# Attention, mixing and expert stages of one network layer on one core: scores and first expert layer in one product, expert table split in two parts, query rows scaled by GpSimd, and a new order on every engine

## What is computed

```
y  = clip(modulated(x, cond) + bias, -256, 256)
q  = l2norm(layernorm(y) @ Wq) * q_scale;  k = l2norm(y @ Wk) * k_scale;  v = y @ Wv     # 16 heads of 64
x1 = x + softmax(8 * q k^T + alibi, causal, 2 null keys) @ v @ Wout
kx = modulated(x1, cond);  A = softmax(kx_h kx_h^T / 4) over the 16 heads of one row
z  = modulated(A kx, cond)
cluster = argmax(calibrate(z @ cluster_sigs^T))             # 8 clusters
tile    = argmax(calibrate(z @ sigs^T) inside cluster)      # 64 experts, 8 to a cluster
h  = gelu(z @ w1 + b1);  comp = tanh(h @ w2 + b2)           # 64 hidden, 2 out
mag = relu(comp @ spline_w1[tile] + spline_b1[tile]) @ spline_w2[tile] + spline_b2[tile]
out = x1 + layernorm(z + mag * directions[tile] * scale) * gamma + beta
```

## Time and profile before

| | |
|---|---|
| median of 3 runs | 1919.03 us (1913.91 to 1920.64) |
| profiled execution | 1920.77 us, of which 1919.0 us are the span from its first to its last instruction |
| PE busy | 1836.4 us (96%) |
| PEld busy | 1489.1 us (78%) |
| DVE busy | 1629.5 us (85%) |
| ACT busy | 1237.6 us (64%) |
| POOL busy | 1065.0 us (56%) |
| chain that ended last | PE 93%, DVE 4%, POOL 1%, ACT 1% |
| granted PE clock | 0.977 of full speed over the span |

### The profile page before, as it was taken

How to read it: one execution, slowest core, us unless ns; L and a number is a source line. 1 busy time by engine, 2 the same in 40 slices (tenths; PEclk the granted TensorE clock), 3 DMA queues, 4 the chain that set the end, 5 groups by cost and what they waited for, 6 DMA issues and landing times.

```text
span 1919.0 us, 63488 instructions
## 1 busy us (share of the span) xinstructions
PE 1836.4 (96%) x25286; PEld 1489.1 (78%) x25286; DVE 1629.5 (85%) x4120; ACT 1237.6 (64%) x2514; POOL 1065.0 (56%) x775
## 2 busy tenths in 40 slices
PE   4899999999999999999999999999999999999974
PEld 3688888878888887887888888788888878878762
DVE  5577888888888899888889888888988988898765
ACT  2566676666667666666766666666666676666642
POOL 0455565565565566556556655655655565565522
PEclk7899999999999999999999999999999999999985
DMA  4011122122112112112211211221121121122121
GB/s 145 9 26 37 41 46 46 40 42 44 39 44 44 37 42 44 44 38 46 42 38 44 44 44 38 41 45 40 44 44 39 40 44 44 38 47 43 44 48 28
DMA packets 337972, 83.09 MB, mean 43 GB/s; under 512 B 277007, under 2 KB 336879, under 8 KB 337903
## 3 DMA queue, kind: packets, MB, share of 16 engines
q1 hardware_dynamic: 337902, 82.12, 19.6%
HBM read 48.51 MB, written 33.55 MB: 43 GB/s over the span
## 4 chain that ended last, share of the span: by engine, by line
PE 93%; DVE 4%; POOL 1%; ACT 1%; issue 1%; SPq 0%; DMA 0%; POOLq 0%; ACTq 0%; DVEq 0%
PE pa L439 29%; PE ps L518 6%; PE pa L446 6%; PE pb L418 6%; PE ps L505 6%; PE ps L469 5%; PE ps L476 4%; PE pc L652 3%; PE pc L538 3%; PE pa L418 3%; PE ps L562 3%; PE pb L425 3%; PE pb L610 3%; PE pb L513 2%; PE ps L520 2%; PE pb L430 2%
## 5 line engine op out<-in xcount | busy, mean ns | idle before, releaser
L1106 POOL TENSOR_TENSOR yve<-ymv,eps 128x1 f32<-128x1 f32 x64 | 12.1, 190 | 547.3 <-DVE ymv L1007 547.3
L439 PE MATMUL pa<-wq,xnTs 128*128 128x512 f32 x768 | 213.4, 414 | 0.0
L439 PE MATMUL pa<-wv,y 128*128 128x512 f32 x768 | 210.4, 410 | 1.9 <-ACT kn L782 0.3
L439 PE MATMUL pa<-wk,y 128*128 128x512 f32 x768 | 211.8, 411 | 0.0
L1098 POOL TENSOR_TENSOR rn<-nrg,mhalf 128x16 f32<-128x16 f32 x64 | 203.4, 3177 | 4.2 <-DVE nrg L1055 3.7
L1086 POOL TENSOR_TENSOR rn<-nrg,mhalf 128x16 f32<-128x16 f32 x64 | 186.6, 2915 | 17.7 <-DVE nrg L1033 11.6
L439 PEld LDWEIGHTS pa<-wv,y 128*128 128x128 f32 x768 | 134.8, 188 | 32.3 <-issue 5.4
L1091 POOL TENSOR_TENSOR bd<-vm,pick 128x1024 f32<-128x1024 f32 x64 | 121.9, 1905 | 65.3 <-PE pc L652 61.5
L439 PEld LDWEIGHTS pa<-wq,xnTs 128*128 128x128 f32 x768 | 137.4, 192 | 24.9 <-ACT kcat L736 0.3
L439 PEld LDWEIGHTS pa<-wk,y 128*128 128x128 f32 x768 | 134.7, 188 | 27.8
L1103 POOL TENSOR_TENSOR pr<-pr,rden 128x1056 f32<-128x1056 f32 x64 | 135.9, 2123 | 2.9 <-DVE rden L927 2.9
(11 more groups left out here) (222 smaller groups left out, 5206.1 us busy)
## 6 DMA issues: line engine op xcount, KB each, us to landing
xT<-in_xT SPq DMA_DIRECT2D x64, 128.0 KB, 2.4
x<-in_x SPq DMA_DIRECT2D x64, 128.0 KB, 2.1
x1d<-x SPq DMA_DIRECT2D x64, 128.0 KB, 1.7
kxdr<-kxn SPq DMA_DIRECT2D x64, 128.0 KB, 1.7
vm<-kxdr SPq DMA_DIRECT2D x128, 64.0 KB, 2.8
odr<-o SPq DMA_DIRECT2D x256, 32.0 KB, 2.0
on<-odr SPq DMA_DIRECT2D x64, 128.0 KB, 2.1
xb<-x1d SPq DMA_DIRECT2D x64, 128.0 KB, 2.1
```

The costliest lines, as they stand in the source:

```text
L439: last = mm(bank, part(lhs(a_, k)), part(rhs(b_, k)), start=(n == 0), stop=(n == 3 * CK - 1))
```

## The change

Four edits of the work, and new lists for all engines:

1. Scores and first expert layer become one product: zT as weights against all 136 columns of `wsc`. The hidden layer is then in rows (`hidn`). For each two tiles PE transposes it once; gelu reads the result with b1 as its bias, and one product with a block-diagonal `w2b` serves both tiles. b2 becomes the bias of two tanh instructions.
2. `gath` is split once, in the setup, into a high and a low part (`gath2`, one column wider, which holds zeros). The product with `ohT` becomes two float32r products.
3. The query rows are scaled by GpSimd, between the two powers.
4. The lists: the q and k products move from tile i-1 to i-2, the attention scores from i-2 to i-3, `kx` from i-4 to i-5, the one-hot and table product from i-8 to i-9, and so on; the low parts of y move from the end of y's own step into the next.

```diff
+        hidn = sb("hidn", [P, 2, CH])
+        hT = sb("hT", [2 * CH, P])
+        gath2 = sb("gath2", [NT, 2, GATH + 1])
...
PE, tile i-7:
-                    for k in range(CK):
-                        mm(pb[:, C:C + NS], zT[:, k, :], wsc[:, k, 0:NS],
-                           start=(k == 0), stop=(k == CK - 1), skip_group_check=True)
-                    for k in range(CK):
-                        last = mm(pb[0:CH, C + P:C + 2 * P], wsc[:, k, NS:NS + CH], zT[:, k, :],
-                                  start=(k == 0), stop=(k == CK - 1), skip_group_check=True)
+                    for k in range(CK):
+                        last = mm(pb[:, C:C + NS + CH], zT[:, k, :], wsc[:, k, :],
+                                  start=(k == 0), stop=(k == CK - 1), skip_group_check=True)
...
+                if live(i, 8):
+                    if p == 1:
+                        nc.tensor.transpose(pb[:, C:C + P], hidn[:, :, :].rearrange("p u h -> p (u h)"), ident[:, :])\
+                            .then_inc(S("hT_mm"), 2)
...
-                        for u in range(2):
-                            mm(pb[:, C + P + 2 * u:C + P + 2 * u + 2], hT[:, u, :], w2b[:, :], start=True, stop=True)
+                    if 1 - p == 0:
+                        mm(pb[:, C + P:C + P + 4], hT[:, :], w2b[:, :], start=True, stop=True)
...
-                    mm(pb[:, 0:GATH], ohT[:, :], gath[:, :], start=True, stop=True).then_inc(S("gathered"), 1)
+                    for a in range(2):
+                        last = mm(pb[:, 0:GATH + 1], part(ohT[:, :]), part(gath2[:, a, :]), start=(a == 0), stop=(a == 1))
...
ACT:
-                    fn(hT[0:CH, 1 - p, :], pb[0:CH, C + P:C + 2 * P], ACT.Identity, bias=b1[:, :]).then_inc(S("hidden"), 1)
+                    fn(hidn[:, 1 - p, :], pb[:, C + NS:C + NS + CH], ACT.Copy).then_inc(S("hidden"), 1)
...
+                    if p == 1:
+                        fn(hT[:, :], pb[:, C:C + P], ACT.Gelu, bias=b1[:, :]).then_inc(S("gelu_done"), 2)
...
+                    if 1 - p == 0:
+                        for o in range(2):
+                            fn(comp[:, :, o], pb[:, C + P:C + P + 4].rearrange("p (u o) -> p o u", o=2)[:, o, :], ACT.Tanh,
+                               bias=b2[:, o:o + 1])
...
DVE:
-                if live(i, 2):
-                    wait(dve, "q_rsqrt", t2)
-                    v.tensor_tensor(by_head(qn), by_head(qn), bc(rn[:, 0, :], 2, DH), ALU.mult).then_inc(S("qn_done"), 1)
...
POOL, after the power of the query norms:
+                    wait(pool, "q_rsqrt", t2)
+                    g.tensor_tensor(by_head(qn), by_head(qn), bc(rn[:, 0, :], 2, DH), ALU.mult).then_inc(S("qn_done"), 1)
+                    wait(pool, "k_guard", t2)
+                    g.tensor_tensor(rn[:, 1, :], nrg[:, 1, :], mhalf[:, :], ALU.pow).then_inc(S("k_rsqrt"), 1)
```

More of the change, by code:

```diff
@@ L355, in step @@
                     sp.dma_start(plain(x1d, t4), x1[:, p, :]).then_inc(D("x1_out", p), 16)
[L356 to L362, removed]
-                    for u in range(2):
[L364 to L372, removed]
+                if live(i, 3):
+                    if live(i, 5):
+                        wait_dma(sp, "x1_out", t5, 1 - p)
+                    sp.dma_start(x1[:, 1 - p, :], plain(x_t, t3)).then_inc(D("x_in", 1 - p), 16)
             pipeline(sp, step)
@@ new lines, in step @@
+                if live(i, 2):
+                    wait(pe, "q1_raw", t2)
+                    project(pa[:, 1, :], lambda a, k: y3f[:, p, a, k, 0:P],
+                            lambda a, k: wk[:, a, k, 1 * 512:2 * 512]).then_inc(S("k1_mm"), 1)
+                if live(i, 3):
+                    for s in range(BT):
+                        last = sim_tile(R7, 1, s)
+                    last.then_inc(S("sim_mm"), 1)
+                if live(i, 6):
+                    wait(pe, "aT_done", t6)
+                    wait(pe, "spread", t6)
@@ new lines, in step @@
+                if live(i, 2):
+                    wait(pe, "q0_raw", t2)
+                    project(pa[:, 0, :], lambda a, k: y3f[:, p, a, k, 0:P],
+                            lambda a, k: wk[:, a, k, 0 * 512:1 * 512]).then_inc(S("k0_mm"), 1)
+                if live(i, 6):
+                    for n in range(G):
+                        for u in range(2):
+                            half, b4, c4 = n % 2, n // 2, 2 * (n % 2) + u
+                            g = half * G8 + b4
+                            at = b4 // QG * P + half * DH + b4 % QG * H
+                            rows = slice(u * DH, (u + 1) * DH)
+                            last = mm(pc[c4 * DP:(c4 + 1) * DP, b4 * DH:(b4 + 1) * DH],
+                                      aT[rows, at:at + DP], vbd[rows, :, g * DM:(g + 1) * DM],
+                                      start=True, stop=True, skip_group_check=True)
+                    last.then_inc(S("av_mm"), 1)
@@ L482, in step @@
+                if live(i, 4):
+                    for r in range(4):
+                        mm(ps[:, 2, C:2 * C], oT[:, r, :], wout[:, r, :], start=(r == 0), stop=False)
+                if live(i, 9):
+                    wait(pe, "ohT_done", t9)
+                if live(i, 7):
+                    linear_T(two(pb, C), wo2, om).then_inc(S("zT_mm"), 1)
                 if live(i, 2):
@@ L541, in step @@
                     last.then_inc(S("mix_scores"), 1)
[L542 to L549 removed]
                 if live(i, 2):
+                    wait(pe, "qT1_done", t2)
@@ L571, in step @@
-                if live(i, 4):
-                    wait(pe, "kxT_done", t4)
-                    from_T(two(pb, 0), kxT).then_inc(S("kxn_mm"), 1)
+                        for t, s in ((0, 0), (1, 1), (1, 0), (0, 1)):
+                            last = pv_tile(r, t, s, 1 - p)
+                    last.then_inc(S("pv_mm"), 1)
                 if live(i, 5):
@@ L681, in _ @@
             loaded(act, "late_in")
+            fn(part(gath2[:, 0, 0:GATH]), gath[:, :], ACT.Copy).then_inc(S("gath_high"), 1)
             act.wait_ge(S("nullw_mm"), 1)
```

620 lines of the change are left out of this document (302 added, 318 removed).

## The result

The changed kernel takes 1999.18 us (median of 4 runs, 1997.54 to 2001.10), the kernel before 1918.44 in the same session. The ratio is 1.0424 (95% interval 1.0402 to 1.0447): 4.2% slower. 1959 was forecast, within a range of 1868 to 2022. The direction held; the loss is 81 us, twice the 40 that were forecast, and just above the likeliest case's own range, 1925 to 1995.

What follows compares the result with a forecast made beforehand. PE bounds the kernel before at 28.15 us a step; DVE would bound the changed one at 29.0. From 1920.8, +47 over 55 steps and -7 at the ends give 1961, as median 1959; range 1868 to 2022.

Steps and rivals of the forecast that it cites:

- the likeliest case: DVE bound, with DVE's subtraction ahead of POOL's query product: 1959 us, own range 1925 to 1995, chance 0.46.
- PE's saving: Per step: fused scores and hidden layer 0.52, expert table 0.29, two-tile hidden layer costs 0.03; together 0.78 us.
- the lock: DVE instructions with two SBUF inputs and POOL instructions reading SBUF, powers excepted, exclude each other; the first holds until it ends.
- (c): After the key-norm power: POOL's division, xb and key rows in a row delay DVE's chain gs to yy by 3.8 us.
- The four places: Spots in the new lists where DVE waits for POOL's holds: 1.2, 0.6, 3.8 and 0.9 us a step.
- DVE's step: 22.5 us without the waits for POOL, 29.0 with them, more than PE's 27.4 and the old 28.15.
- The step that failed: Filling and draining steps: DVE and POOL seldom collide, PE's saving counts for some nine tiles, -7 us.
- PE stayed the bound: Rival: DVE's waits add up to less than 4.9 us, PE's saving shows, 1869 us (1860 to 1890); chance 0.23.
- The race at (b): After q_guard, DVE's subtraction leads POOL's query product by 0.1 us; rival: POOL first, +1.3 a step, 2031 or 1995; chance 0.17.
- The powers: Rival: GpSimd's powers, which read SBUF, hold DVE up too; 253 us more, about 2210; chance 0.01.
- (a): After y_mv: POOL's spread holds 1.89 us and DVE stands 1.2 us before the division of the mixing weights.

Runs made afterwards that it cites:

- run 5: Kernel before, in its own order, plus both product edits and nine small products in PE's set-up that move its loop: 1876.83 us, ratio 0.9780.
- run 8: Changed kernel with the old expert-table product (two passes of 321 columns) put back: 2002.89 us, ratio 1.0437.
- run 1: Changed kernel with GpSimd's softmax division, addition of beta and key-row scaling replaced by powers of about the same length: 1890.21 us, ratio 0.9857.
- run 7: Changed kernel with GpSimd's xb and key rows held until VectorE has copied the null keys, in the first 12 steps only: 1994.30 us, ratio 1.0395.
- run 9: Changed kernel with xb and key rows held until the null-key copy, and the spread until the one-hot rows are written: 1925.03 us, ratio 1.0034.
- run 10: Changed kernel with only GpSimd's spread held until VectorE has written the one-hot rows: 1987.48 us, ratio 1.0359.
- run 6: Changed kernel with GpSimd's xb and key rows held in every step until VectorE has copied the null keys: 1960.03 us, ratio 1.0212.
- run 4: Kernel before, in its own order, with only the scaling of the query rows moved to GpSimd: 1938.88 us, ratio 1.0114.
- run 11: Kernel before with 55 repeats of a small product in PE's set-up, which move its otherwise unchanged loop: 2089.99 us, ratio 1.0894.

## Why the prediction was right in direction and short in size

1. *PE's saving.* Forecast 0.52 + 0.29 - 0.03 = 0.78 a step; the pieces measured 0.60 and 0.24. Where PE is the bound it is worth 0.65 a step (run 5), and in after next to nothing (run 8). Right.
2. *DVE becomes the bound through the lock.* Shown by run 1, where GpSimd is as busy and as late but holds nothing at (c), and the time falls by 109 us. The four places are where they were laid out and sum to 6.0 against 6.5.
3. *DVE's step.* Forecast 22.5 + 6.5 = 29.0; measured 29.15. With 6.0 of waits, 22.5 leaves 0.65. Of this, 0.54 are DVE's wait for the exponentials (0.64) and one that the profile puts down to issue (0.43), each in every second step, which the forecast held at nothing. The growth of a step is right within 0.19 (1.04 against 0.85), which over the 51 steps from tile 12 to 63 is 9.5 us of the miss (52.9 against 43.4).
4. *The step that failed*, by its size, is "In the filling and draining steps the lock seldom meets, and PE's saving counts for some nine tiles: -7." Measured, the ends are 16.5 + 10.3 = 26.8 us longer than before. The first half is wrong: by run 1 the lock accounts for 16.2 + 6.5 of them, and run 7 finds some 9 of the filling at `xb` and the key rows alone. The second half is wrong for the new lists: with the lock of (c) gone (run 1), tile 12 still comes 0.3 us later than before and the end takes 3.8 longer, so nothing of PE's saving shows there. It does in the old lists, where run 5 takes 5.5 and 7.7 us less, counted from tile 0's statistics and tile 63's. The prediction gives no reason for "seldom". The filling step of after that is shown under run 7 speaks against it: two instructions let go by the same end start together however empty the rest is, and there PE stood for 3.31 us behind the one that lost. The term measured +27 instead of -7. With it, the same sum gives 1921 + 47 + 27 = 1995, for an execution that took 2000.
5. *Rivals.* PE stayed the bound in none of the new lists except with the lock at (c) gone (run 1, PE busy 98.3% from 800 to 1100 us) or, in part, moved (run 9, 97.0%). The race at (b) did not turn in after (the subtraction starts at 1027.29, the query product at 1027.47), but it turned in runs 9 and 10, in each second step, when the spread was moved: a lead of 0.1 to 0.2 us is worth a rival. The powers didn't hold VectorE up, again.
6. *What the forecast left out.* Lock waits were added up as if each were paid in full. Taken out one at a time they aren't: (a) alone gives 0.22 a step of its 1.3 (run 10), (c)'s last two holds alone 0.44 of their 2.0 (run 6), both together 1.26 of 3.3 (run 9, where PE is the bound in the odd steps and waits for the held spread in the even ones).

The parts, each measured in the old lists: products -43 us (run 5), query rows +20 (run 4). Added, -23. After is +81. So about 100 us come from the new order of the lists together with these edits. That the sum may be taken like this is an assumption; no run has the new lists without any of the edits. Open is also what makes the end of the span 3.8 us longer even without the lock at (c) (run 1), and whether a GpSimd power would hold the lock if it had as much to read as a product.

## What to carry to other kernels

Moving an elementwise operation from VectorE to GpSimd isn't priced by its duration or by how idle GpSimd is, but by which VectorE instructions stand beside it in time. Lay both lists side by side, look for holds that follow one another, and keep them from a chain of short dependent instructions, each of which may wait for a whole hold. Do the same for the filling and draining steps, where two waiters of one releaser meet with nothing else to do. When you hold an instruction back to free one engine, look who waits for its result. And when an edit changes the number of TensorE's instructions, look at the instruction queue's packets first: a loss at the start of each round can come from the loop's place and not from the work.

## What the runs showed of the hardware that was not expected

- TensorE's loop stood at its start in every round or in none, depending on its place in the instruction stream, with the loop itself unchanged: 9 packets of 16 KB a round, 4.5 to 4.7 us of standing in the mean, the clock at 0.73 for some 9 us behind it, together 6.6 to 6.7 us a round. 36 instructions more ahead of the loop took it away (run 5), 220 more brought it about (run 11, whose page counts 110 more on PE and 110 more on PEld for the 55 repeats).
- A wait of 1.93 us of TensorE was followed by 6 us at a granted clock of 0.77 and 0.66 (run 6), one of 1.42 by none in after.
- GpSimd's powers of up to 16 elements, which read and write SBUF, didn't hold VectorE up in run 1, not even three in a row; its division, its products, the spread and the sum of 256 elements did in after.
